# Making a selective scan's inputs one at a time on GpSimd, and moving VectorE's small jobs between the slots of a fused attention, scan and mixture-of-experts kernel

## The reference, cut to what matters

```python
def layer(x, ctx):
    # 1. cross attention, 16 heads of 16, over 1601 keys a batch; qdq rounds to int8 steps
    q = qdq(layernorm(x)) @ qdq(wq).T + bq
    k, v = split(ctx @ wkv.T + bkv)
    x = x + qdq(softmax(q @ k.T / 4) @ v) @ qdq(wp).T + bp
    # 2. selective scan over the 64 tokens of a batch, 16 states for each of 256 channels
    n = layernorm(x)
    dt_low, b, c = split(n @ x_proj_w.T)
    dt = softplus(dt_low @ dt_proj_w.T + dt_proj_b)
    h[t] = exp(dt[t] * a) * h[t - 1] + (dt[t] * n[t]) * b[t]
    x = x + sum(h * c, states) + n * D_param
    # 3. mixture of experts: 64 experts, the best 8 for a token, capacity 512
    x = x + moe(layernorm(x))
```

## Time and profile before

| | |
|---|---|
| median of three runs | 2181.81 us (2178.58 to 2183.49) |
| the profiled execution, its own time | 2179.32 us |
| its span | 2177.5 us |
| TensorE busy, matrix products | 2005.8 us, 92% |
| VectorE busy | 1747.0 us, 80% |
| ScalarE busy | 1610.5 us, 74% |
| GpSimd busy | 614.7 us, 28% |
| mean granted TensorE clock | 0.973 |

### The profile page before, as it was taken

How to read it: one execution, slowest core, us unless ns; L and a number is a source line. 1 busy time by engine, 2 the same in 40 slices (tenths; PEclk the granted TensorE clock), 3 DMA queues, 4 the chain that set the end, 5 groups by cost and what they waited for, 6 DMA issues and landing times. The chain is left out here.

```text
span 2177.5 us, 52408 instructions
## 1 busy us (share of the span) xinstructions
PE 2005.8 (92%) x19018; PEld 1569.9 (72%) x19018; DVE 1747.0 (80%) x3649; ACT 1610.5 (74%) x3269; POOL 614.7 (28%) x604
## 2 busy tenths in 40 slices
PE   6999999999999999999999999999997469989966
PEld 5777777777777777777777777777774358878854
DVE  6558898989898989898888889898978747767746
ACT  4778787878787878787878878787877247767743
POOL 0002030303122121313030403030312147767760
PEclk9999999999999999999999999999999579999988
DMA  6888783434334343434343434343421156766738
GB/s 200 284 283 284 238 288 116 140 97 126 117 96 141 73 139 86 130 93 128 94 128 83 137 79 131 82 135 82 139 73 52 62 172 215 218 217 218 221 117 347
DMA packets 189535, 330.04 MB, mean 152 GB/s; under 512 B 37771, under 2 KB 154167, under 8 KB 183136
## 3 DMA queue, kind: packets, MB, share of 16 engines
q1 hardware_dynamic: 170848, 291.99, 44.3%
q0 software_dynamic: 18432, 34.69, 4.3%
HBM read 165.53 MB, written 108.27 MB: 126 GB/s over the span
## 5 line engine op out<-in xcount | busy, mean ns | idle before, releaser
L859 ACT ACTIVATE sb_probsT<-W 128x384 f32<-128x384 f32 (+1 forms) x1024 | 476.7, 517 | 89.5 <-PE W L673 84.6
L1050 DVE TENSOR_REDUCE sb_negmax<-S 128x1 f32<-128x1608 f32 x256 | 468.3, 1829 | 72.3 <-PE S L663 69.6
L867 ACT ACTIVATE sb_probs<-S,sb_negmax 128x1608 f32<-128x1608 f32 x256 | 410.3, 1603 | 92.4 <-DVE sb_negmax L1050 91.6
L673 PEld LDWEIGHTS W<-sb_ident,sb_probs 128*128 128x128 f32 (+1 forms) x3328 | 358.1, 139 | 159.4 <-ACT sb_K_f L851 105.7
L673 PE MATMUL W<-sb_ident,sb_probs 128*128 128x128 f32 (+1 forms) x3328 | 465.1, 278 | 3.9 <-ACT sb_probs L867 2.0
L1440 POOL DMA_INDIRECT y_scratch<-sb_ys,sb_places x256 | 252.1, 985 | 109.3 <-issue 72.5
L851 ACT ACTIVATE sb_K_f<-W,sb_k_cols 128x402 f32<-128x402 f32 x256 | 153.6, 600 | 152.5 <-PE W L636 152.3
L663 PE MATMUL S<-sb_K,sb_Q 32*128 32x402 f32 (+1 forms) x2048 | 243.5, 546 | 13.1 <-ACT sb_probs L867 10.2
L691 PE MATMUL O<-sb_probsT,sb_V 128*32 128x128 f32 (+1 forms) x6656 | 244.1, 277 | 0.0
L549 POOL TENSOR_TENSOR sb_bx<-sb_u,sb_BC 128x512 f32<-128x512 f32 x120 | 172.5, 1459 | 209.2 <-DVE sb_z L1124 190.4
L691 PEld LDWEIGHTS O<-sb_probsT,sb_V 128*32 128x32 f32 (+1 forms) x6656 | 173.5, 109 | 47.4 <-issue 37.3
(11 more groups left out here) (209 smaller groups left out, 3585.1 us busy)
## 6 DMA issues: line engine op xcount, KB each, us to landing
sb_ctx<-ctxT SPq DMA_DIRECT2D x128, 402.0 KB, 4.0
sb_K<-sb_K_f SPq DMA_DIRECT2D x1024, 50.2 KB, 1.9
xe_scratch<-sb_none SPq DMA_DIRECT2D x32, 1088.0 KB, 5.4
sb_xg<-xe_scratch SPq DMA_DIRECT2D x64, 544.0 KB
sb_BC<-bc_scratch SPq DMA_DIRECT2D x32, 1024.0 KB
sb_Q<-sb_q_own SPq DMA_DIRECT2D x128, 128.0 KB, 3.4
y_scratch<-sb_none SPq DMA_DIRECT2D x16, 1024.0 KB, 5.5
sb_rows<-y_scratch SPq DMA_DIRECT2D x16, 1024.0 KB, 8.5
```

Of the source, the lines that this page charges most:

```text
L673: ins = pe.transpose(W[0:keys_in(t), at * P:(at + 1) * P], probs[n % 2][:, t * P:t * P + keys_in(t)], ident[:])
L859: act.activation(probsT[k][n % (k + 1)][:, 0:wide], ring[bank_of("T", G, k)][:, 0:wide], ACT.Copy)\
L867: act.activation(probs[n % 2][:].rearrange("p (c k) -> p c k", c=QUADS), scores_of, ACT.Exp, bias=negmax[:, slot:slot + 1], accum_out=den[ ...
L1050: dve.tensor_reduce(negmax[:, slot:slot + 1], scores_of, AX.XY, ALU.max, negate=True).then_inc(max_done, 1)
```

## The change

It does five things.

1. GpSimd makes the scan input of unit `u` only when the scores of slot 9 + `u` are done (`scan_at`, a wait on `s_done`), one a slot; before, units 0 to 3 came back to back. `part_q` now stands behind unit 1 instead of unit 3.
2. The low parts of the context move to other slots of VectorE (`LOW_AT`): those of slots 4, 7 and 10 go to 5, 8 and 12, slot 8 has two of them, and 11 keeps one (of another quarter). `LOAD_AT`, when SyncE issues the loads that reuse the buffer, moves with them.
3. `round_q` moves from slot 7 to slot 8.
4. `moments_q` moves within slot 1, ahead of `rest_b`.
5. The job `O0` moves from slot 10 to slot 8, behind `XQ`; its `norm_o` so moves from the start of slot 11 to that of slot 9.

The number of instructions on each engine stays; no computation changes.

```diff
-LOAD_AT = {2: (2, 0), 3: (2, 1), 4: (2, 2), 5: (2, 3), 8: (3, 0), 9: (3, 1), 11: (3, 2), 12: (3, 3)}
+LOW_AT = {1: ((1, 0),), 2: ((1, 1),), 3: ((1, 2),), 5: ((1, 3),), 8: ((2, 0), (2, 1)), 11: ((2, 2),), 12: ((2, 3),)}
+LOAD_AT = {2: (2, 0), 3: (2, 1), 4: (2, 2), 6: (2, 3), 9: (3, 0), 10: (3, 1), 12: (3, 2), 13: (3, 3)}
...
-       (8, 2): ["XQ"], (9, 2): ["Q"], (10, 2): ["O0"], (14, 2): ["O1"], (1, 0): ["yT"], (1, 2): ["O2"],
+       (8, 2): ["XQ", "O0"], (9, 2): ["Q"], (14, 2): ["O1"], (1, 0): ["yT"], (1, 2): ["O2"],
...
+def lows_at(G):
+
+    i, slot = divmod(G, SLOTS)
+    return [(2 * i + ahead, c) for ahead, c in LOW_AT.get(slot, ()) if 2 * i + ahead < BATCHES]
+
+
+def scan_at(p, unit):
+
+    return min((p + 1) * SLOTS + LAG + FIRST_DECAY + 1 + unit, ALL_STRIPS - 1)
...
+                pool.wait_ge(s_done, scan_at(p, unit) + 1)
                 mine = slice(q * QS, (q + 1) * QS)
...
-                    for unit in range(UNITS // 2):
+                    for unit in range(2):
                         scan_input(i - 1, unit)
                 if nxt:
                     part_q(i + 1)
                 if prev and i < PAIRS:
-                    for unit in range(UNITS // 2, UNITS):
+                    for unit in range(2, UNITS):
                         scan_input(i - 1, unit)
...
-                if slot == 7 and nxt:
+                if slot == 8 and nxt:
                     round_q(q_link)
+                if slot == 5:
+                    for low in lows_at(G):
+                        part_low(*low)
+                if slot == 1 and nxt:
+                    q_link = moments_q(i + 1)
...
-                if part_at(G, PART_AT):
-                    part_low(*part_at(G, PART_AT))
+                if slot != 5:
+                    for low in lows_at(G):
+                        part_low(*low)
...
-                if slot == 1 and nxt:
-                    q_link = moments_q(i + 1)
```

## The result

The changed kernel took 2206.66 us (median of 4 runs, 2204.14 to 2209.62) against 2182.65 of the kernel before on the same chip: a ratio of 1.0117, 95% interval 1.0104 to 1.0130. It is slower by 24 us, where 2151 was forecast with a range up to 2172. The profiled execution took 2209.62 us.

A forecast was written before the change was run, and what follows sets the result against it. It took TensorE to be bound by waits for a late VectorE: 9.1 + 12.0 + 7.0 + 1.8 = 29.9 us less gave 2151.9 as a median, stated as 2151 with a small gap; range 2138 to 2172.

The forecast's parts named there:

- One input a slot: Slots 9 on: inputs beside the maxima shorten slot 9's recurrence by 1.77 us; 9.1 us won, 1.8 in the last pair.
- the wait for `q_out`: Slot 10: TensorE's product for the values waits for VectorE's copy, 9.1 us in 11 times; all of it goes.
- `O0` to slot 8: Slot 11: the values no longer stand behind `norm_o`, so that wait of 12.0 us over the span goes.
- the 7.0 us of slot 2: Slot 2: with the moments earlier in slot 1, VectorE reaches `norm_o` 0.68 us sooner; the whole wait goes.
- What comes to slot 8: Slot 8: added work fits VectorE's waits, slot 9's maximum stays to 0.1 us; no gain, no cost.
- Low parts to 11 and 12: Slots 11 to 13: VectorE's 6.38 us a slot against TensorE's 6.0 makes it late, at a cost taken as 0.
- Two such slots make VectorE 0.8 us late by slot 13: Slots 11 and 12, each with values, a unit and a low part, leave VectorE 0.8 us late; cost taken as 0.
- The low part in slot 5: Slot 5: it goes ahead of a step waiting for TensorE's product; cost taken as 0, at most 0.9 us a pair.
- The rival with its chance of 0.06: VectorE's tail: inputs tied to the scores get between additions and hold the next 1.25 us; near 2240 us, chance 0.06.
- it needs to be late by more than the last instruction: VectorE's tail: argument against the slower rival, that holds need VectorE later than its last instruction's length; chance 0.06.
- the threshold at two hits a pair: VectorE's tail: the slower rival decides from two holds a pair on, 2 x 1.25 against 2.1 us won.

The follow-up runs named there:

- 5: Kernel before, each scan input waiting for VectorE's last instruction with two SBUF operands in the slot before, mask behind unit 1, no moves: 2168.93 us.
- 8: 5 with two moves only, `O0` from slot 10 to 8 and the moments ahead in slot 1: 2156.37 us.
- 4: Changed kernel, each input waiting for VectorE's last instruction with two SBUF operands in the slot before instead of the scores: 2157.68 us.
- 9: 4 with `round_q` back in slot 7: 2153.67 us.
- Experiment 2: Kernel before with GpSimd's part of the change alone (wait for the scores, mask behind unit 1's input): 2210.55 us.
- Experiment 6: 4 with a further GpSimd product in each of the eight units, after the unit's scan, written to an unread scratch tile: 2259.8 us.
- 7: 4 with a GpSimd memset of a scratch tile in each of the eight units, after the unit's scan: 2158.35 us.
- 3: Changed kernel with GpSimd's part as before (four inputs back to back, no wait for the scores, mask behind unit 3): 2226.11 us.
- 1: Changed kernel without GpSimd's wait for the scores, all moves kept: 2197.51 us.

## Why the prediction was wrong

**One input a slot.** Right: all scans at 1.23 us, the wait for `q_out` gone, 10.9 us forecast and 11.9 measured where the inputs can do no harm (5).

**`O0` to slot 8, and the 7.0 us of slot 2.** The waits went, but the size was off: 19.0 us forecast, 12.6 measured (8 against 5). Slot 11 gave 0.90 us a pair, 12.6 in all, for 12.0 forecast. Slot 2 gave 0.35 a pair, from 7.54 to 7.19 us, 4.9 for the 7.0 forecast. And slot 8, with `O0` and the first low part still ahead of its maximum, grew from 7.39 to 7.67, which takes 3.9 back.

**What comes to slot 8.** Right in sum: with the whole table (4) slot 8 gave 0.44 us and slot 9 took 0.38. The forecast had the maximum of slot 9 where it was, to 0.1 us; it came 0.4 later behind its scores. `round_q` gains nothing by leaving slot 7, as said, but costs in slot 8: 4.0 us (9).

**Low parts to 11 and 12, and the moment of each input. This is the step that failed: a late VectorE was taken to cost nothing.** The prediction let each input start with the scores, "which is when the maximum starts if VectorE is on time". It found that "Two such slots make VectorE 0.8 us late by slot 13", took the lateness seen in slots 10 and 11 of the kernel before as proof that being late is free, and wrote "I take 0". The runs showed 58 us of holds in its place, of which 49 reach the time (the change against 4). (The low part in slot 5 cost nothing, as taken: slots 4 to 6 of TensorE are as before to 0.01 us.) Being late was free as long as GpSimd's inputs hung on VectorE's own progress. The change hangs them on the scores, and then a late VectorE is hit. The lateness itself was worked out nearly right: in 4, where nothing is held, the maxima of slots 12 to 0 start 2.00, 2.20, 1.74, 1.81 and 1.54 us behind their scores' issue where 1.03 is on time, so 0.5 to 1.2 late. The values' copy, which waited 0.47 us for its product in slot 11 (at 942.61 in the changed kernel), was missing from VectorE's 6.38 us.

But the moved low parts are not what makes VectorE late. Experiment 2 has them in their old places and is as slow. The lateness of the earlier trace rows was read as the work of the 3.00 us scan. That was right for slot 10, whose maximum is on time in 5 (1.03 us); but with that scan gone and nothing held (5), slot 11's maximum still comes 1.4 us late (2.46 less 1.03), slot 12's 1.0 and slot 15's and 0's 0.5.

**The rival with its chance of 0.06 is what happened**, by the mechanism that it named: issued while VectorE's additions run, in between two of them, the next one held. It set the threshold at two hits a pair; there were 3.9. It gave 8.8 us of VectorE's a pair for seven hits; it was 4.2 (58.3 us in the groups of low parts, L1131, L1137 and L1133, over 14 pairs). What kept its chance small was the sentence "it needs to be late by more than the last instruction". That was no argument against: the last instructions are 0.29 us, and the lateness that the same text worked out was 0.8.

Behind it stood one open question, whether GpSimd gets the port between two of VectorE's instructions that follow each other at once. Experiment 6 answers it: it does in 105 of 105 times in which its product stands waiting, and the holds are of 1.00 us there in the mean and of 1.08 in the changed kernel (58.3 us in 54). The Trainium skill (SBUF — State Buffer, "Who interferes with whom") says that the one that issues first has the shared pair for the whole instruction, and that it is GpSimd's reading of SBUF that contends; 6 and 7 agree on both. By the order of issue alone, though, the recurrence at 914.74 of the earlier trace rows would have gone ahead of GpSimd's last input, and it did not.

The sum, redone with what was measured, from 2181.9: 11.9 + 12.6 us won (5, 8), 1.3 lost by the low parts and `round_q` (4 against 8), which makes 2158.7 (4 measured 2157.7). Then 58.3 us of holds. How much of them reaches the time is not worked out but read from the two times: 49.0, which leads from 4 to 2206.7.

## What to carry to other kernels

When work of GpSimd that reads SBUF is given a new trigger, ask what VectorE does at that moment when it is late, not when it is on time: tie it to VectorE's last instruction with two operands in SBUF, so that it always falls beside a reduction or a copy out of PSUM. An engine that runs late for free is only free while nothing else is timed by the engine that it lags behind. And where a price decides between faster and slower and no row has it, its chance should be that of the condition, which could be worked out, and not that of surprise.

## What was not expected of the hardware

- A GpSimd product that waits at the end of a VectorE instruction goes in ahead of VectorE's next (6: 105 of 105 times), while VectorE did not get in between the products of a row of four: one low part of 0.99 us took 5.84 (3). It isn't always so: in 14 pairs of 1 a recurrence did get in between two products, and in three pairs of the changed kernel slot 11's low part went ahead of the input. What decides is open.
- A GpSimd memset of 128x512 (0.53 us) beside VectorE's product with two operands in SBUF costs it nothing (7).
- A stall of TensorE of some 4 us cost more than its length: the mean granted clock of the next 6 us was 0.62, with a stretch at 1.2 GHz in place of 2.4 (3).
